# Where ScalarE runs exp and the row squares, and where VectorE combines rows, in a fused attention and mixture-of-experts kernel

## The reference, cut to what matters

```python
h = _attention(_rms(x, ln1_w[l]), wq[l], wk[l], wv[l], wo[l], cos, sin, causal_bias)
x = clip(x + h, -100, 100)             # 16 heads of 64, 4 key/value heads, rope, causal softmax
logits = _rms(x, ln2_w[l]) @ wr[l]     # 8 experts, each row goes to its 2 best
out = sum over the 2 chosen e of comb[e] * ((silu(h @ wg[e]) * (h @ wu[e])) @ wd[e])
x = clip(x + out, -100, 100)
```

## Time and profile before

| | |
|---|---|
| median of 3 runs | 3653.08 us (3648.91 to 3657.68) |
| profiled execution: time, span | 3653.33 us, 3651.5 us |
| busy: PE, DVE, ACT, POOL | 80%, 60%, 55%, 51% of the span |
| mean granted clock of TensorE | 0.906 of full speed |
| main loop | from 230 us to 3440 us, 42 to 58 us for an iteration |

### The profile page before, as it was taken

How to read it: one execution, slowest core, us unless ns; L and a number is a source line. 1 busy time by engine, 2 the same in 40 slices (tenths; PEclk the granted TensorE clock), 3 DMA queues, 4 the chain that set the end, 5 groups by cost and what they waited for, 6 DMA issues and landing times.

```text
span 3651.5 us, 69801 instructions
## 1 busy us (share of the span) xinstructions
PE 2906.2 (80%) x22326; PEld 2366.8 (65%) x22326; DVE 2193.6 (60%) x8164; ACT 2016.6 (55%) x7089; POOL 1858.4 (51%) x1671
## 2 busy tenths in 40 slices
PE   5238887888888887888888987888888988888673
PEld 2226666777667766777667766777667766777462
DVE  5775555665556655665556665666566665666343
ACT  3026666566655665665656565656566665656321
POOL 0035655444655466554655556554655565555413
PEclk9569999999999999999999999999999999999775
DMA  9110101443145421543245421453145411442374
GB/s 375 74 41 31 35 33 59 146 150 122 52 133 175 153 84 61 169 148 117 67 136 169 155 78 61 164 165 97 67 137 179 163 56 62 153 154 80 115 251 137
DMA packets 270444, 438.36 MB, mean 120 GB/s; under 512 B 36305, under 2 KB 155633, under 8 KB 268657
## 3 DMA queue, kind: packets, MB, share of 16 engines
q1 hardware_dynamic: 253696, 400.31, 33.1%
q0 software_dynamic: 16384, 33.59, 3.0%
HBM read 323.13 MB, written 110.62 MB: 119 GB/s over the span
## 4 chain that ended last, share of the span: by engine, by line
PE 58%; ACT 19%; DVE 10%; POOL 6%; issue 3%; DMA 2%; SPq 1%; POOLq 0%; DVEq 0%
ACT arena L1030 10%; PE psum L759 7%; PE psum L777 7%; PE psum L807 5%; PE psum L808 4%; PE psum L809 4%; PE psum L734 4%; PE psum L779 3%; PE psum L827 3%; ACT arena L1037 3%; PE psum L877 3%; PE psum L878 2%; PE psum L879 2%; PE psum L903 2%; PE psum L902 2%
## 5 line engine op out<-in xcount | busy, mean ns | idle before, releaser
L1264 POOL TENSOR_TENSOR arena<-arena 128x512 f32<-128x512 f32 (+1 forms) x512 | 744.0, 1475 | 729.6 <-DVE arena L1558 727.7
L1030 ACT ACTIVATE arena<-arena 128x128 f32<-128x128 f32 (+1 forms) x2048 | 901.0, 446 | 23.6 <-DVE arena L1553 23.6
L759 PE MATMUL psum<-arena 128*128 128x128 f32 x3072 | 475.5, 292 | 259.0 <-ACT arena L1037 230.7
L759 PEld LDWEIGHTS psum<-arena 128*128 128x128 f32 x3072 | 342.9, 145 | 373.0 <-ACT arena L1037 293.4
L1037 ACT COPY arena<-psum 128x384 f32<-128x384 f32 x1024 | 445.5, 480 | 237.7 <-PE psum L759 236.7
L1562 DVE COPY arena<-psum 128x512 f32<-128x512 f32 x256 | 177.1, 692 | 618.4 <-PE psum L779 616.3
L734 PE MATMUL psum<-arena 64*128 64x128 f32 (+1 forms) x4096 | 453.5, 365 | 0.1
L1549 DVE CUSTOM_DVE_ANT_0 arena<-psum,arena 128x256 f32<-128x256 f32 x1024 | 430.2, 420 | 0.0
L807 PE MATMUL psum<-h_hi,wqk_hi 128*128 128x256 f32 x1280 | 392.8, 307 | 45.2 <-DVE arena L1549 43.7
L1527 DVE TENSOR_TENSOR arena<-psum,arena 128x512 f32<-128x512 f32 x640 | 406.0, 681 | 26.2 <-PE psum L809 21.3
L1280 POOL TENSOR_TENSOR arena<-arena 128x512 f32<-128x512 f32 x320 | 400.6, 1278 | 8.7 <-DVE arena L1527 8.6
(11 more groups left out here) (199 smaller groups left out, 5711.0 us busy)
## 6 DMA issues: line engine op xcount, KB each, us to landing
gu<-gu_kept SPq DMA_DIRECT2D x320, 512.0 KB, 4.3
wd<-wd_kept SPq DMA_DIRECT2D x320, 256.0 KB, 3.9
arena<-rows_in SPq DMA_DIRECT2D x320, 64.0 KB
rows_out<-arena SPq DMA_DIRECT2D x320, 64.0 KB
rows_in<-arena SPq DMA_DIRECT2D x34, 512.0 KB, 7.8
rows_out<-arena SPq DMA_DIRECT2D x34, 512.0 KB, 7.1
gu_kept<-w_hi SPq DMA_DIRECT2D x32, 256.0 KB
gu_kept<-w_lo SPq DMA_DIRECT2D x32, 256.0 KB
```

Source lines behind the costliest of these rows:

```text
L759: mm = T.transpose(psum[:, t_bank(key), j * P:(j + 1) * P], probs[:, q, i, j * P:(j + 1) * P], ident)
L1030: ins = A.activation(a, a, ACT.Exp, bias=negmax[:, q, k:k + 1], accum_out=rowsum[:, q, k:k + 1])
L1264: ins = G.tensor_tensor(a, a, r[:, :, t:t + 1].broadcast_to([P, 4, P * (t + 1)]), ALU.mult)
```

## The change

On ACT, `exps(it, 0)` moves ahead of place 1. `square_rows(it + 1)` and `exps(it, 1)` stand directly behind `copy_probs(it - 1, 3)`, in this order, ahead of `copy_v` and place 2. `exps(it, 2)` moves up to stand ahead of `copy_routed`, place 4 and `copy_probs(it, 0)`. `exps(it, 3)` moves ahead of place 7. On DVE, `combine(it + 1)` moves ahead of `copy_o(it - 1, 3)` and place 2. No instruction is added or taken away.

```diff
@@ ScalarE @@
                 if old:
                     copy_probs(it - 1, 2)
+                if now:
+                    exps(it, 0)
                 place(it, 1)
-                if now:
-                    exps(it, 0)
                 if old:
                     copy_probs(it - 1, 3)
-                if now:
+                if coming:
+                    square_rows(it + 1)
+                if now:
+                    exps(it, 1)
                     copy_v(it)
                 place(it, 2)
-                if now:
-                    exps(it, 1)
-                if coming:
-                    square_rows(it + 1)
                 place(it, 3)
...
                 if now:
                     round_piece(it)
+                    exps(it, 2)
                 if old:
                     copy_routed(it - 1)
                 place(it, 4)
...
                 place(it, 5)
-                if now:
-                    exps(it, 2)
                 place(it, 6)
...
                     copy_ranks(it - 1)
+                if now:
+                    exps(it, 3)
                 place(it, 7)
-                if now:
-                    exps(it, 3)
@@ VectorE @@
                     invert(it, 0)
+                if coming and it + 1 >= B:
+                    combine(it + 1)
                 if old:
                     copy_o(it - 1, 3)
                 place(it, 2)
-                if coming and it + 1 >= B:
-                    combine(it + 1)
```

More of the change, by code:

```diff
@@ L1146, in _ @@
                     copy_probs(it - 1, 2)
-                place(it, 1)
                 if now:
                     exps(it, 0)
+                place(it, 1)
                 if old:
                     copy_probs(it - 1, 3)
+                if coming:
+                    square_rows(it + 1)
                 if now:
+                    exps(it, 1)
                     copy_v(it)
                 place(it, 2)
-                if now:
-                    exps(it, 1)
-                if coming:
-                    square_rows(it + 1)
                 place(it, 3)
@@ L1186, in _ @@
                     copy_ranks(it - 1)
-                place(it, 7)
                 if now:
                     exps(it, 3)
+                place(it, 7)
             for hs in range(HS):
```

## The result

The changed kernel takes 3740.9 us (median of 4 runs, 3733.8 to 3745.7) against 3655.3 us of the kernel before beside it: a ratio of 1.0235 (95% interval 1.0211 to 1.026), 2.35% slower. The forecast was 3746 us, slower. The profiled execution took 3736.7 us, span 3734.9; that of before 3653.3 and 3651.5.

A forecast was written before the change was run, and what follows sets the result against it. PE was taken to set the pace (58% of the chain), with ACT costing time where PE waits for it. Iteration terms of +84 us and 9 us for the clock on 3653 gave 3746 us, range 3656 to 3785.

The forecast's parts named there:

- part 3: Squares, exp of group 1 and `combine` moved up: the large one, with exp now queued behind the gathered rows.
- Part 1: Exp of group 0 ahead of place 1: free on ACT, 2.0 us earlier in iteration 27, spent again by the gate.
- Part 2: Exp of group 3 ahead of place 7: gains 0.2 us where 2.2 was expected; 1.0 us at `u = 6`.
- x: Time DVE has clipped the combined rows; iteration 27: 1548.0 with middle landing, 1545.25 if nothing holds it, 1548.8 with late landing.
- rival A: Gathered rows land early, in 2.5 us, x near 1545.3: 3657 us, up to 3685; chance 0.12 above 3660.
- Gate at +1.7 us: Gate product of place 3, iteration 27, starts at 1553.7 in place of 1551.97: +1.7 us (-1.0 to +2.5).
- `u` = 7 and 0 at +2.2 and +2.3: Iterations without a tile at place 2: later `turn_h`, six of each kind from 15 on, +13 and +14 us.
- The clock at +9 us: PE's slower clock behind waits, now ahead of the longer output projection: 9 us lost, bounds 0 and 18.
- Rival C: Slower clock bites in tiles' iterations too, 1 us in each of 24 more: 3779 us; chance 0.09.
- Part 4: Exp of group 2 ahead of `copy_routed`: +0.6 us at even place 4, nothing without tiles there.
- B: Faster: PE never waits at places 2 and 3 in tiles' iterations, so gains are kept: 3616 us; chance 0.07.
- D: No change that can be measured, gains and losses cancel: 3653 to 3660 us; chance 0.06.

The follow-up runs named there:

- parts 1 and 3 together: Kernel before with exp of group 0 ahead of place 1, squares and exp of group 1 early, `combine` ahead of `copy_o`: 3781.4 us, ratio 1.0055.
- part 2 alone: Kernel before with only `exps(it, 3)` moved ahead of place 7: 3639.8 us, ratio 0.9958.
- `invert` late: Changed kernel with `invert(it, 0)` behind `combine` on DVE: 3706.9 us beside the changed kernel, 3701.3 us on another chip; ratios to before 1.0153 and 0.9833.
- the first of the four edits: Kernel before with only `exps(it, 0)` moved ahead of place 1: 3533.6 us, ratio 0.9673.

## Why the prediction was right

The direction, the place of the loss (part 3, over late rows and `combine`) and, to within 0.9 us, the forecast for iteration 27 are borne out. That the sum came out within 6 us is in part luck: terms missed by up to 32 us cancel, and the clock went the other way than priced.

- **Part 1 is free and then spent.** Shown. Alone it gives 120 us; parts 1 and 3 together are slower than before. In iteration 27 the copies of group 3 are on time after the change (the gap before the second half of the group is 0.24 us, it was 2.02), and the gate of place 3 is late all the same. Its worth alone was mis-sized, since the clock was left out: 48 of 113 us are granted clock.
- **Part 2 gains 0.2 us, not 2.2.** Right for iteration 27, where the run of part 2 alone has 0.25 us less wait. Its 14 us are clock, and the prediction missed the wait of 1.94 us that part 2 brings at `u = 5`, 14 us over seven iterations; the changed kernel has it in each of them.
- **Part 3 and x.** The clip was forecast at 3.15 us behind the start of the v projection, by 5 us of landing and `combine` ending 1.07 us behind `normalise`. It ends at 3.5, with a landing of 4.2 us and exactly that 1.07. Over the 24 iterations with `u` = 2 to 5 from 15 on, the rows landed 4.0 to 5.6 us after the last gather's start, 4.8 in the mean, so the 5 us taken from iteration 25 was sound. (That exp ran before "while the gathered rows were still on their way" holds for `u = 1`, but not for iteration 27: there DVE no longer waited for them, and exp ran beside `combine`.) POOL's hold was given too much: `combine` takes 1.26 or 1.27 us in 13 of the 24 and above 2 us in one, where it was to take above 2. In those 13 the landing alone holds x. In the others, and at `u = 6`, POOL does: 3.52 us against 1.26 there, where 21 of the 36 us of `invert` late lie. The Trainium skill, page "SBUF — State Buffer", section "SBUF: two separate sides", says that a VectorE instruction with two SBUF inputs and a GpSimd one that reads SBUF shut each other out; the trace agrees, with 3.52 us against 1.26. None of the 24 landed in the 2.5 us of rival A. The Trainium skill, page "DMA: Bandwidth & Descriptors", section "Queues, rings and completion order", says that each DMA engine takes turns between its queues by packets; that did not bring these rows early.
- **Gate at +1.7 us.** It was +2.6 against the old distance (9.7 less 5.1, less the 2.0 of part 1). The chain over ACT and DVE would have allowed 1542.64 + 5.7 = 1548.3; PE came at 1548.86, when its own output projection was done, which took 4.84 us at a granted clock of 0.76 and not 3.74. That is the step that was too small in the prediction: the projection "is done by x + 5"; the gate behind it came at x + 6.2. That is 0.5 us; nearly all of the rest is x, at 3.5 us and not 3.15.
- **`u` = 7 and 0 at +2.2 and +2.3.** Less than half of what came: the intervals grew by 5.1 and 4.8. Two reasons in the trace of 31: the rows are there at 1763.05, 4.8 us behind the v projection's start where before it was 1.9, and the projection takes 5.29 us. The prediction kept x where it was, 4.6 us behind the v projection; it came 6.4 us behind. The last gather starts 1.2 us later against the v projection, and lands in 4.35 us, not 2.66, with the DMA engines busy for 0.62 of that stretch and not 0.25. In iterations 39 and 55 the rows land in 2.5 to 2.6 us, and `turn_h` still comes 11.9 us behind the v projection and not 7.7: the later gather and the slow projection are enough.
- **The clock at +9 us.** The wrong sign in total. The projection alone is 72 us longer in busy time (312.2 against 240.0), and the other matmuls are 94 us shorter, since PE's busy time fell by 22 us in all (2906.2 to 2884.4). Rival C falls with it.
- **Iterations 0 to 8.** -21 forecast, -19.9 measured. **Part 4** +17 forecast, nothing measured alone.
- **The sum** held (92 forecast, 84 measured in the main loop) because the kinds with tiles lost less than forecast by 24 us and `u` = 7 and 0 more by 32, 9 to 14 gained 7 more, and the 9 of the clock did not come by itself. **Rival A** is refuted by the landings, and by iteration 30: even when DVE's first instruction gets ahead of `normalise`, the others wait it out. **B** and **D** fall with it.
- **The signs.** Those named came, but for three: `combine` above 2 us; ACT's wait of some 3 us for the clip, which is 5.6 us in the mean (270.2 in 48); and the waits of L759 for L1037, which fell by 128 us and not 60, since part 2 also takes its 2.2 us out of them and puts 1.5 before L866.

## What to carry to other kernels

In an engine's fixed order, a step that waits for another stage's data must not be put ahead of long work that waits for nothing: exp of group 1 had run beside the landing or the combining of the gathered rows, and with the squares ahead of it, it waited for both, in 48 iterations. Move one step at a time: the first of the four edits was worth 3.3%, and the third took it all away. Work out every kind of iteration: the wait at `u = 5` did not show in the one that was read closely. Before a wait is moved earlier, look at when its data land in each kind of iteration, and at who runs beside it on the ports it uses.

## What the runs showed of the hardware

- Four VectorE instructions with two SBUF operands took 3.52 us beside POOL's 2.95 us of SBUF work and 1.26 without it, and this also when VectorE started first (1715.86 against 1716.03).
- Work behind a long wait of TensorE is slow: 32 matmuls took 3.74 to 3.75 us without a wait ahead, 4.84 us behind one of 2.91 us (granted clock 0.76, between the levels 1.2 and 2.4 GHz), 5.29 us behind 6.00 us (0.70). Removing 65 us of short waits gave 48 us more of busy time back.
- From the start of the last of four indirect gathers to their landing it took 2.5 to 2.8 us with a DMA share of 0.18 to 0.25 (iteration 31 before: 2.66 us at 0.25), 4.35 us at 0.62 (31 after), 4.0 to 5.6 us in the 24 iterations with tiles after the change (27: 4.23 us at 0.87), and 5.45 us at 1.00 (25 after). One landing of before does not fit (iteration 32: 3.58 us at 0.17).
- One of the chips ran the kernel before in 3762 us and another in 3654, while another kernel took 3701 and 3707 us on them. The cause is open.
